# Gated cross attention: the split context tiles are kept in DRAM for the later head groups

## What is computed

```python
q = layernorm(x) @ Wq.T                   # 32 heads of 32
k, v = context @ Wk.T, context @ Wv.T     # interleaved per head
q, k = rmsnorm(q), rmsnorm(k)             # per head
x = x + tanh(g_xattn) * softmax(q k^T / sqrt(32)) v
h = sigmoid(n @ Q(w1).T) * (n @ Q(w2).T)  # n = layernorm(x); Q: ternary weights
x = x + tanh(g_ffn) * (h @ Q(w3).T)
```

## Time and profile before

| | |
|---|---|
| median of 3 runs | 2548.94 us (2546.76 to 2552.81) |
| the profiled execution | 2549.59 us, span 2547.5 us |
| granted TensorE clock, mean | 0.969 |
| busy: PE, PEld | 95%, 56% of the span |
| busy: DVE, ACT, POOL | 63%, 58%, 34% |
| DMA | 386 MB, mean 152 GB/s |

### The profile page before, as it was taken

The page is one execution under the profiler, slowest core; times in us unless marked ns, Lnnn a source line. Parts: engine busy times, 40 slices in busy tenths (PEclk is TensorE's granted clock), DMA queues, the critical chain, the costliest instruction groups (busy, mean ns, idle before and its releaser), DMA issues.

```text
span 2547.5 us, 49407 instructions
## 1 busy us (share of the span) xinstructions
PE 2411.4 (95%) x18386; PEld 1420.8 (56%) x18386; DVE 1598.3 (63%) x2660; ACT 1480.6 (58%) x3038; POOL 862.3 (34%) x811
## 2 busy tenths in 40 slices
PE   7998999999999999999999887747999999999999
PEld 5874566666666666666665544434555555544444
DVE  5665788888888888888888767764444444320000
ACT  5664898988989989999887766742111111110000
POOL 3663345444454444444446555461000000000000
PEclk9998999999999999999999988758999999999999
DMA  6775565656555665565655666666323233243451
GB/s 236 241 220 185 151 155 146 158 146 186 150 155 147 156 178 157 146 160 142 160 142 148 180 180 179 156 189 211 106 96 114 92 109 110 91 126 98 150 157 50
DMA packets 281231, 386.02 MB, mean 152 GB/s; under 512 B 114336, under 2 KB 223392, under 8 KB 276256
## 3 DMA queue, kind: packets, MB, share of 16 engines
q1 hardware_dynamic: 280992, 382.86, 53.2%
HBM read 276.75 MB, written 56.89 MB: 131 GB/s over the span
## 4 chain that ended last, share of the span: by engine, by line
issue 33%; PE 32%; POOL 30%; DMA 2%; DVE 1%; POOLq 1%; ACT 1%; SPq 0%; DVEq 0%; ACTq 0%
PE ps L1515 21%; POOL krs L680 13%; PE ps L1542 10%; POOL oinv L698 6%; POOL qrs L642 3%; POOL kms L675 3%; POOL osum L696 2%; POOL oatt L704 2%; DMA stage<-x_normalised 1%; POOL cn L726 1%; POOL oinv L700 1%; POOL qms L639 1%; POOLq L60 1%; DVE plo L1247 0%; DMA attention<-oatt 0%
## 5 line engine op out<-in xcount | busy, mean ns | idle before, releaser
L1415 PE MATMUL ps<-wk,chi 128*128 128x512 f16 x3072 | 926.6, 383 | 4.8 <-DVE clo L1130 3.3
L1415 PE MATMUL ps<-wk,clo 128*128 128x512 f16 x1536 | 588.6, 383 | 0.0
L1247 DVE TENSOR_TENSOR plo<-pf,phi 125x448 f16<-125x448 f32 x768 | 511.9, 669 | 97.1 <-ACT phi L915 93.3
L924 ACT ACTIVATE pf<-ps 125x448 f32<-125x448 f32 x768 | 417.0, 543 | 143.3 <-PE ps L1433 128.5
L1515 PE MATMUL ps<-xnTh,w12q 128*128 128x512 f16 (+1 forms) x1408 | 480.9, 355 | 3.8 <-ACT xnTh L940 3.8
L1515 PE MATMUL ps<-xnTl,w12q 128*128 128x512 f16 (+1 forms) x1408 | 480.4, 355 | 0.0
L915 ACT ACTIVATE phi<-pf 125x448 f16<-125x448 f32 x768 | 443.7, 578 | 5.3
L1415 PEld LDWEIGHTS ps<-wk,chi 128*128 128x128 f16 x3072 | 252.8, 97 | 200.7 <-issue 16.0
L1457 PE MATMUL ps<-val,phi 125*128 125x65 f16 x3072 | 283.5, 193 | 56.4 <-DVE plo L1247 56.2
L680 POOL TENSOR_TENSOR krs<-kms,mhalf 125x8 f32<-125x8 f32 x192 | 325.5, 1695 | 15.0
L1130 DVE SCALAR_TENSOR_TENSOR clo<-craw,csc,chi 128x1000 f16<-128x1000 f32 x193 | 258.2, 1338 | 111.4 <-ACT chi L847 111.4
(11 more groups left out here) (113 smaller groups left out, 2958.0 us busy)
## 6 DMA issues: line engine op xcount, KB each, us to landing
craw<-in_ctx SPq DMA_DIRECT2D x193, 500.0 KB, 4.6
gbuf<-in_wffn SPq DMA_DIRECT2D x33, 1024.0 KB, 6.8
wraw<-in_wffn SPq DMA_DIRECT2D x66, 512.0 KB, 5.8
kst<-kpair SPq DMA_DIRECT2D x128, 250.0 KB, 7.8
cstream<-in_ctx SPq DMA_DIRECT2D x48, 500.0 KB, 4.5
hid<-hidden SPq DMA_DIRECT2D x7, 2816.0 KB, 12.5
hidden<-hh SPq DMA_DIRECT2D x66, 256.0 KB, 2.1
kst<-kpair SPq DMA_DIRECT2D x128, 125.0 KB, 2.5
```

What stands on the lines that cost most here:

```text
L924: act.activation(pf[0:KW, e % 6, :], bank(3 + e % 3)[0:KW, 0:2 * S], ACT.Exp, bias=LN128, scale=SCALE).then_inc(p_ready, 1)
L1247: dve.tensor_tensor(plo[0:KW, e % 6, :, :], pf[0:KW, e % 6, :].rearrange("p (t n) -> p t n", t=2), phi[0:KW, e % 6, :, :], ALU.subtract).t ...
L1415: mm = pe.matmul(bank(pt)[:, :], a[:, pt, kc, :], wkp[g % 2][:, w, kc, :], start=(kc == 0 and n == 0), stop=(kc == KC - 1 and n == 2))
```

## The change

A DRAM tensor `cp_d` holds the 48 split tiles, 512 KB each (both parts, with the padding to 128 columns). `chi` and `clo` with two buffers each become `cpair` with four buffers of a high and a low part, 8 KB more per partition. In the first group (T < 48) tiles are loaded and split as before, and SP stores the pair of tile T - 3 right after it issues the load of tile T; the last three are stored at T = 48, where SP waits until all stores have landed. ACT's split of tile T waits for the store of tile T - 4 and the projection of T - 4, in place of that of T - 2. From T = 48 on `load_ctx` loads the pair, when the projection of tile T - 4 is over, PE waits for its landing, and neither ACT nor DVE splits anything. The load and split of one tile past the end are gone.

```diff
@@ -63,6 +63,7 @@
 def flamingo_kernel(nc, x_d, ctx_d, wq_d, wkv_d, wffn_d, gates_d, out_d):
     qst_d = nc.dram_tensor("q_pairs", [G, NP, P, TOK], F16, kind="Internal").ap()
     att_d = nc.dram_tensor("attention", [U, S, GC], F32, kind="Internal").ap()
+    cp_d = nc.dram_tensor("ctx_pairs", [NC, P, 2, KC, P], F16, kind="Internal").ap()
     cn_d = nc.dram_tensor("x1_normalised", [TOK, 2, D], F16, kind="Internal").ap()
     x1_d = nc.dram_tensor("x_after_attention", [TOK, D], F32, kind="Internal").ap()
     hid_d = nc.dram_tensor("hidden", [P, FJ, 2, TOK], F16, kind="Internal").ap()
@@ -127,8 +128,7 @@
         wk1 = sb(ab, "wk1", [P, 2, KC, 512], F16)
         wkp = (wk0, wk1)
         wkraw = sb(ab, "wkraw", [P, KC, 512], F32)
-        chi = sb(ab, "chi", [P, 2, KC, P], F16)
-        clo = sb(ab, "clo", [P, 2, KC, P], F16)
+        cpair = sb(ab, "cpair", [P, 4, 2, KC, P], F16)
         cjunk = sb(ab, "cjunk", [P, KC, KW], BF16)
         wjunk = sb(ab, "wjunk", [P, 2, 512], BF16)
 
@@ -228,6 +228,8 @@
         wk_in = sem("wk_in"); wkhi_ready = sem("wkhi_ready"); wklo_ready = sem("wklo_ready")
         ctx_in = [sem(f"ctx_in{i}") for i in range(3)]
         stream_in = [sem(f"stream_in{i}") for i in range(4)]
+        pair_in = [sem(f"pair_in{i}") for i in range(4)]
+        pair_saved = [sem(f"pair_saved{i}") for i in range(4)]
         cssq_ready = sem("cssq_ready"); csum_ready = sem("csum_ready"); cfr_ready = sem("cfr_ready")
         csc_ready = sem("csc_ready"); ctab_step = sem("ctab_step")
         wssq_ready = sem("wssq_ready"); wsum_ready = sem("wsum_ready"); wfr_step = sem("wfr_step")
@@ -386,10 +388,25 @@
                     for n in stream_tiles(i + 1, c):
                         load_stream(n)
 
+            def save_pair(T):
+                sp.wait_ge(clo_ready, T + 1)
+                sp.dma_start(cp_d[T, :, :, :, :], cpair[:, T % 4, :, :, :]).then_inc(pair_saved[T % 4], 16)
+
             def load_ctx(T, slot, idx):
 
-                wait(sp, clo_ready, T - 2)
-                sp.dma_start(craw[:, slot, :, :], ctx_d[idx, :, :, :]).then_inc(ctx_in[slot], 16)
+                if T < NC:
+                    wait(sp, clo_ready, T - 2)
+                    sp.dma_start(craw[:, slot, :, :], ctx_d[idx, :, :, :]).then_inc(ctx_in[slot], 16)
+                if 3 <= T < NC:
+                    save_pair(T - 3)
+                if T >= NC:
+                    if T == NC:
+                        for n in range(3):
+                            save_pair(NC - 3 + n)
+                        for i in range(4):
+                            sp.wait_ge(pair_saved[i], 16 * (NC // 4))
+                    sp.wait_ge(kv_ready, T - 3)
+                    sp.dma_start(cpair[:, T % 4, :, :, :], cp_d[idx, :, :, :, :]).then_inc(pair_in[T % 4], 16)
 
             tiles_of_x(sp, step_a)
 
@@ -484,7 +501,6 @@
                                 sp.wait_ge(gsum_ready, u * 2 - 2)
                             sp.dma_start(gbuf[:, par, :, :], wffn_d[u, :, :, :]).then_inc(gw_in[par], 16)
                 if k == U:
-                    load_ctx(U * KT, 0, 0)
                     stack_k(U - 1, 0)
                     sp.wait_ge(gsum_ready, 2 * U - 2)
                     sp.dma_start(gbuf[:, 0, :, :], wffn_d[U, :, :, :]).then_inc(gw_in[0], 16)
@@ -615,13 +631,13 @@
             pool.memset(mone[:, :], -1.0).then_inc(consts_ready, 1)
             pool.memset(lneps[:, :], LN_EPS).then_inc(consts_ready, 1)
             pool.memset(rmseps[:, :], DH * RMS_EPS).then_inc(consts_ready, 1)
-            pool.memset(chi[:, :, :, KW:P], 0.0).then_inc(consts_ready, 1)
-            pool.memset(clo[:, :, :, KW:P], 0.0).then_inc(consts_ready, 1)
+            for i in range(4):
+                pool.memset(cpair[:, i, :, :, KW:P], 0.0).then_inc(consts_ready, 1)
             pool.wait_ge(pool_step, 2)
             for m in (ident, identh):
                 pool.affine_select(out=m[:, :], in_=m[:, :], compare_op=ALU.not_equal, fill=1.0, base=0,
                                    pattern=[[-1, P]], channel_multiplier=1).then_inc(consts_ready, 1)
-            pool.wait_ge(consts_ready, 9)
+            pool.wait_ge(consts_ready, 11)
 
             def x_rstd(i, par):
 
@@ -843,8 +859,9 @@
 
             def ctx_high(T, par, slot, use):
                 act.wait_ge(ctx_in[slot], use)
-                wait(act, kv_ready, T - 1)
-                act.activation(chi[:, par, :, 0:KW], craw[:, slot, :, :], ACT.Copy,
+                wait(act, kv_ready, T - 3)
+                wait(act, pair_saved[T % 4], 16 * (T // 4))
+                act.activation(cpair[:, T % 4, 0, :, 0:KW], craw[:, slot, :, :], ACT.Copy,
                                scale=csc[:, T % NC:T % NC + 1]).then_inc(chi_ready, 1)
 
             act.wait_ge(csc_ready, NC // CB)
@@ -877,7 +894,7 @@
                                        ).then_inc(ksq_ready, 1)
                         if t != 1:
                             value_high()
-                    if j == 1 and projects(k):
+                    if j == 1 and projects(k) and u * KT + t + 1 < NC:
                         tn = par * KT + t + 1
                         slot = tn % 3
 
@@ -1127,8 +1144,8 @@
 
             def ctx_low(T, par, slot):
                 dve.wait_ge(chi_ready, T + 1)
-                dve.scalar_tensor_tensor(out=clo[:, par, :, 0:KW], in0=craw[:, slot, :, :],
-                                         scalar=csc[:, T % NC:T % NC + 1], in1=chi[:, par, :, 0:KW],
+                dve.scalar_tensor_tensor(out=cpair[:, T % 4, 1, :, 0:KW], in0=craw[:, slot, :, :],
+                                         scalar=csc[:, T % NC:T % NC + 1], in1=cpair[:, T % 4, 0, :, 0:KW],
                                          op0=ALU.mult, op1=ALU.subtract).then_inc(clo_ready, 1)
 
             ctx_low(0, 0, 0)
@@ -1322,7 +1339,7 @@
 
         @block.tensor
         def _(pe):
-            pe.wait_ge(consts_ready, 9)
+            pe.wait_ge(consts_ready, 11)
 
             def x_transpose(i):
                 pe.wait_ge(xn_ready, i + 1)
@@ -1403,7 +1420,10 @@
                     if projects(k):
 
                         if j == 0:
-                            pe.wait_ge(clo_ready, T + 1)
+                            if T < NC:
+                                pe.wait_ge(clo_ready, T + 1)
+                            else:
+                                pe.wait_ge(pair_in[T % 4], 16 * ((T - NC) // 4 + 1))
                             if k >= 1 or t >= 2:
 
                                 wait(pe, khat_ready, T - 1)
@@ -1411,8 +1431,8 @@
                         if r == 0 and b == 0:
                             pe.wait_ge(wklo_ready, KC * (g + 1))
                         for kc in (2 * j, 2 * j + 1):
-                            for n, (a, w) in enumerate(((chi, 0), (chi, 1), (clo, 0))):
-                                mm = pe.matmul(bank(pt)[:, :], a[:, pt, kc, :], wkp[g % 2][:, w, kc, :],
+                            for n, (a, w) in enumerate(((0, 0), (0, 1), (1, 0))):
+                                mm = pe.matmul(bank(pt)[:, :], cpair[:, T % 4, a, kc, :], wkp[g % 2][:, w, kc, :],
                                                start=(kc == 0 and n == 0), stop=(kc == KC - 1 and n == 2))
                         if j == 3:
                             mm.then_inc(kv_ready, 1)
```

## The result

The changed kernel takes **2535.78 us** (median of 5 runs, 2533.17 to 2539.95), the kernel before beside it 2548.94 (2545.96 to 2552.81): ratio 0.995, 95% interval 0.9936 to 0.9965. It is faster by 13 us. Its profiled execution took 2535.29 us, span 2533.4, against 2549.59 and 2547.5 before.

What follows compares the result with a forecast made beforehand. PE was taken to bound some 26 of 32 units, the layer-norm tiles' one-slot store-and-load chain units 27 to 31. 2549.6 - 14 (tail) + 4 (stores) + 0.5 (tile 48) = 2540.1 us; forecast's own range 2530 to 2550, overall 2516 to 2562.

Steps and rivals of the forecast that it cites:

- gain of the tail: Units 27 to 31, with layer norm woven in: four terms saving 14 us together, bounds 0 and 24.
- The splits of groups 1 to 3 lie beside PE: Units 8 to 26: removed ACT and DVE split work is hidden under a busy PE, so 0 us.
- Short halves: Late units, odd LN load to the next even one: ACT's high copy starts earlier, 2.0 us each, four times, 8 us.
- Long halves: Late units, even LN load to odd one, PE waiting for kst: 0.3 us saved each, five times, 1.5 us.
- Unit 27's first tile: Start of unit 27, DVE behind by two clo: first LN tile leaves 2 us earlier, bounds 0 and 3.4.
- After the last load: After the last LN load: PE restarts one clo earlier, perhaps without a clock fall; 2.5 us saved, bounds 0 to 4.8.
- The stores, 4 us: First group: 48 stores in SP's in-order queue, 1.8 us each, delay kst; 4 us lost, bounds 0 and 30.
- The turn at tile 48: At tile 48 SP stores the last three tiles, waits, then loads: 0 to 1 us lost, 0.5 taken.
- Kst in groups 1 to 3: Plain units: first kst part some 1.5 us later behind a gated load, but landing some 4 us before use: 0.
- nothing comes back: Rival, chance 0.15: PE keeps every matmul and the LN chain is DMA landings and POOL work; 2550 us.
- The stores make PE wait: Rival, chance 0.17: units 1 to 7, second kst part late by about 3 us, clock halves; 2578 us.
- The tail frees itself more: Rival, chance 0.15: late units' plo waits get too short for clock falls, 21 us more come back; 2519 us.

Runs made afterwards that it cites:

- The runs with one instruction each: Changed kernel with one split instruction per tile of groups 1 to 3 done for nothing: DVE's alone 2546.02 us, ACT's alone 2538.63 us.
- two slots: Layer-norm tiles of units 27 to 31 alternate between two memory slots, loads ahead of stores: 2499.05 us on the changed kernel, 2511.26 on the kernel before.
- gbuf early as well: Changed kernel with a second layer-norm slot and, in late units, gbuf issued at t = 0 instead of t = 2: 2489.26 us.
- two small moves in SP's order of issues: Changed kernel, late units only: gbuf issued at t = 0 instead of t = 2, 2526.51 us; or first kst part before the LN load, 2523.32 us.

## Why the prediction was right, and where not

2540 was predicted and 2535.8 measured, inside the forecast's own range of 2530 to 2550; the sum's two halves (gain of the tail, cost of the stores) came out as 14.1 us in the profiled execution and nothing, where 14 and 4.5 stood. That the tail met its 14 to the tenth is in part luck, since its four terms came out as 6.8, 1.3, 2.1 and 3.9 for 8, 1.5, 2 and 2.5. Step by step:

- **The splits of groups 1 to 3 lie beside PE: 0 us.** Right. PE fills the plain unit's 42.4 us as before, and 96 splits put back cost nothing. ACT and DVE went down by 5.3 and 6.6 us a unit where 7 and 8 were forecast, and over the whole program by 127 and 166 us where 164 and 194 had been counted; why the rest of their work shows longer was not followed.
- **Short halves, 4 x 2.0 = 8 us.** They gave 6.8: 2.3, 0.5, 2.5 and 1.5. The mechanism was right in the main, in one of its two reasons. The copy does come earlier: DVE's norm starts 15.3 us after the load as it did (15.5 before, by the earlier trace rows), ACT's high copy 16.1 us after it, where it had been 18.9:

```profile
1504.99 0.81 DVE L1142 TENSOR_SCALAR cx<-ca,cag,crs 112x1024 f32<-112x1024 f32 x1 [1.29 <-POOL crs L737]
```

```profile
1505.83 1.06 ACT L858 ACTIVATE cn<-cx 112x1024 f16<-112x1024 f32 x1 [1.21 <-DVE cx L1142]
```

  The text put that down to two things, a chi on ACT and the clo in front of plo. The runs with one instruction each leave the clo: with ACT's back the copy is 0.3 us later at most, and the halves are about as short as without. That the four halves gave unlike amounts comes from the kernel before: its copy stood 3.2, 1.6, 3.4 and 2.5 us behind the norm's start, where it now always stands 0.8. PE's wait for plo is down to 1.49 us, as the prediction had it (1.5).
- **Long halves, 5 x 0.3 = 1.5 us.** 1.3 in all, for the reason given: kst, with the same bytes ahead of it, ends its wait 19.6 us after the LN load (1514.33 to 1533.96, the wait for it now 6.1 us), as it had (1521.52 to 1541.33, 19.8).

```profile
1533.96 0.63 PE L1453 MATMUL ps<-qT,kst 128*125 128x224 f16 x2 [6.11 <-DMA kst<-kpair]
```

- **Unit 27's first tile, 2 us.** Not between the tile's load and its store: that half is 31.1 us in both. The first load was 2.1 us earlier instead. Of this some 0.6 us had been gathered by PE before 1303 us; the remainder goes with the store of an output that stands ahead of the load in SP's program, which left at 1342.0 instead of 1344.1. POOL had begun that output 1.7 us sooner (1338.32 in place of 1339.98), since DVE's sums for the `krs` ahead of it came 1.4 us sooner (1335.94 in place of 1337.31), and had needed 0.4 us less for it. So DVE was less behind, as the prediction said, but the size was right by luck and the place wrong.
- **After the last load, 2.5 us.** It gave 3.9, within its bounds of 0 to 4.8; 2.4 of them by the next LN load, with the clock at 0.91 in the 20 us behind the last load where it had been 0.83, as the text had thought possible. The other 1.5 us were not followed.
- **The stores, 4 us.** The one step that failed. It took a store for 1.8 us of a queue that lands in order and was full. In order it was: in unit 5 of the changed kernel nine transfers issued between 454.0 and 474.1 (the four DMAs of a kst part counted as one) landed in the order of issue (458.8, 460.1, 462.5, 463.7, 465.1, 470.1, 471.3, 474.0, 476.6 us). The Trainium skill (DMA: Bandwidth & Descriptors, Queues, rings and completion order) has descriptors of a ring consumed in ring order, but does not promise that whole DMAs complete in that order; here they did. But the queue was not full. gbuf landed at 462.5 behind a store, and at 462.7 without; the last transfer ahead of the second kst part at 474.0 with three stores more, and at 472.7 without them, 1.3 us for three stores where the prediction had 5.4. That kst part was issued at 472.2 and landed at 476.6, before at 472.6 and 477.0, so it lost nothing. Two readings were wrong. The 8.8 us of the load of 463.9 were read as time that further bytes would lengthen; but what stood ahead of it was kst, in small packets at some 205 GB/s, and two of the three stores had gone through before, where the queue had room. And the 291 GB/s of the earlier trace rows were read as the most the queue moves; the changed kernel moved 408 over 7 us, and the kernel before itself 416 in the microsecond from 1504. The sentence of the prediction that had the stores at zero and the time at 2536 came out in the number, though not by its condition: the order was kept.
- **The turn at tile 48, 0.5 us.** PE waited for nothing there.
- **Kst in groups 1 to 3, 0 us.** Right: between 216 and 1340 PE waited for the first split, 3.3 us, and for nothing else of note.

Of the rivals, "nothing comes back" fell with its reason. The prediction had the Trainium skill's rule to begin with the engine of highest occupancy (Perfetto Trace Analysis, Identifying the Most-Contended Engine) speak against the change. That was half a reading: for TensorE the same section sets matmul busy time aside and takes MFU (the share of peak FLOPs) and the busy share of the weight loads. The latter is 56% here, below DVE's 63%; MFU was not worked out, so the rule in full gives no clear verdict. What the change took from PE was its waits, and the run with DVE's instruction put back shows that they were DVE's. "The stores make PE wait" came true at three stores a tile, not at one. "The tail frees itself more" did not come in this kernel: the clock in 1340 to 1600 was 0.90 before and 0.91 after. It came in the kernels that cut the chain, 0.96 with two slots and 0.97 with gbuf early as well. What would have shown the forecast wrong were stretched units of group 0, a late kst in plain units, or long halves below 31 us; none of them came, save for one long half of 30.7.

Open: why the copy of the kernel before stood less far behind the norm in its second short half than in the others; and how the 12 us of the change under two slots divide between DVE and ACT, which was tried with one slot only.

## What to carry to other kernels

Price engine time by the stage: splits of 164 us on ACT and 194 on DVE gave 14 us, because 26 of 32 units stand on another engine, and the stage with a chain gave all of it; an experiment that does the removed instruction for nothing, on one engine at a time, finds the engine in two runs. Before a DMA is given a price in a queue, compare the rate that the queue moves now, microsecond by microsecond, with the highest it shows anywhere in the trace: as long as it is below, and the packets are not small ones, a store between loads may cost nothing. Neither a long landing time nor a high DMA share alone is proof that more bytes would come later. When the removed work was the cover of another wait, here kst, that wait is the next thing to change, and two small moves in SP's order of issues gave 9 and 12 us on top, nearly the change's own 13, and a second slot for the chain 37.

## What the hardware showed that was not expected

**The DMA share does not tell how much more the queue can move.** One core's queue moved 189, 252 and 344 GB/s in 25 us, with zero, one and three stores a tile (in unit 5, and in the kernel with three stores in unit 4, which is there at the same place of its program), and the share went from 0.81 to 0.88 and 1.04. Within these 25 us it moved 408 GB/s at a share of 1.01 and 210 at 1.14; at the latter most packets were under 2 KB.

**SP's issues get longer where the queue is full.** With three stores a tile, SP's issue of three stores took 1.4 to 6.1 us in 400 to 500, where a single store of the changed kernel took 0.4 to 1.7, and 0.4 most often. That the full queue is what holds SP is likely; no run separates it:

```profile
464.86 6.09 SPq L396 DMA_DIRECT2D ctx_pairs<-cpair  x3
471.05 2.63 SPq L470 DMA_DIRECT2D kst<-kpair  x4
```

**Some of POOL's instructions are shorter when DVE has less to do.** POOL was busy for 814 us in place of 862 with the same work, and 30 of these 48 us are in one instruction, the reciprocals `oinv` (mean 2338 ns before, 1870 after); `krs` stayed as it was (1695 and 1708). The reciprocals in 1207 to 1292, kernel before, DVE's split alone done for nothing, ACT's alone, and the changed kernel (the mean in ns stands behind the busy time):

```profile
L698 POOL TENSOR_TENSOR oinv<-oraw,mone 128x8 f32<-128x8 f32 x5 | 11.8, 2364 | 0.0
```

```profile
L722 POOL TENSOR_TENSOR oinv<-oraw,mone 128x8 f32<-128x8 f32 x5 | 10.9, 2178 | 0.0
```

```profile
L722 POOL TENSOR_TENSOR oinv<-oraw,mone 128x8 f32<-128x8 f32 x5 | 9.0, 1791 | 0.0
```

```profile
L714 POOL TENSOR_TENSOR oinv<-oraw,mone 128x8 f32<-128x8 f32 x4 | 6.5, 1634 | 0.0
```

The one instruction stretched from 1.6 to 2.4 us beside the split, more by DVE's than by ACT's. It shows that they go together, not through what. Of the first LN load's 2.1 us only some 0.4 rest on that.
